# Cross-attention with a routed expert layer: four early expert tiles taken from six routed token tiles instead of three from four, with a new instruction order

## The reference

```
x1 = x + attention(layernorm(x), ctx, mask) @ Wo + bo
h = layernorm(x1)                                  # 1024 x 128
probs = softmax(h @ w_gate + b_gate)               # 8 experts
p, e = max(probs), argmax(probs)
out = x1 + p * (relu(h @ W1[e] + b1[e]) @ W2[e] + b2[e])   # 128 -> 512 -> 128
```

| tokens routed | tokens of expert 0 to 7 | full tiles of 128 with one expert |
|---|---|---|
| first 4 tiles (512) | 140, 9, 31, 132, 9, 8, 9, 174 | 3 |
| first 6 tiles (768) | 140, 9, 39, 323, 13, 44, 24, 176 | 4 |
| all 8 tiles (1024) | 147, 9, 64, 465, 19, 54, 88, 178 | 5 |

## Time and profile before

### The profile page before, as it was taken

One profiled execution on the slowest core, in us unless ns is written; L12 is line 12 of the kernel. 1 busy time (PEld: TensorE's weight loads), 2 busy tenths in 40 slices (PEclk: granted clock), 3 DMA queues, 4 the chain that ended last, 5 costly groups with the idle time before them and its releaser, 6 DMA issues.

```text
span 122.6 us, 2830 instructions
## 1 busy us (share of the span) xinstructions
PE 99.6 (81%) x770; PEld 79.4 (65%) x770; DVE 74.3 (61%) x255; ACT 75.4 (62%) x377; POOL 53.7 (44%) x85
## 2 busy tenths in 40 slices
PE   4599899979799999999888889986319999799700
PEld 4376665426558888856785579975209999689600
DVE  0551687664869979569766766567725266656600
ACT  0603855998579998789895998545003675474300
POOL 7730003067009683063886324152780056467560
PEclk9999999999999999999999999999955899999995
DMA  2999999999999930000010200000142222200010
GB/s 80 350 350 263 288 275 275 275 276 212 373 353 293 298 133 3 0 0 5 14 55 22 66 8 0 22 22 8 47 108 69 66 69 58 71 29 14 23 34 5
DMA packets 17624, 15.06 MB, mean 123 GB/s; under 512 B 1288, under 2 KB 14772, under 8 KB 17600
## 3 DMA queue, kind: packets, MB, share of 16 engines
q1 hardware_dynamic: 16096, 11.99, 37.9%
q10 hardware_dynamic: 704, 1.70, 3.8%
q0 software_dynamic: 800, 1.10, 2.8%
HBM read 8.92 MB, written 6.19 MB: 123 GB/s over the span
## 4 chain that ended last, share of the span: by engine, by line
PE 46%; DVE 14%; issue 10%; ACT 9%; POOL 7%; DMA 7%; DVEq 1%; ACTq 1%; POOLq 0%; SPq 0%
PE bank L996 11%; ACT probs L694 8%; PE bank L876 6%; PE bank L973 6%; PE bank L1191 5%; POOL out_x L570 4%; DMA w_qkv<-in_L_xattn_Wk 4%; PE bank L982 4%; PE bank L923 3%; PE bank L948 3%; PE bank L886 2%; DMA regions<-token_rows,row_of 2%; PE bank L970 2%; DVE neg_max L1468 1%; DMA vo<-regions 1%
## 5 line engine op out<-in xcount | busy, mean ns | idle before, releaser
L694 ACT ACTIVATE probs<-bank,neg_max 128x64 f32<-128x64 f32 x128 | 38.0, 346 | 2.6 <-DVE neg_max L1468 1.9
L694 ACT ACTIVATION_READ_ACCUMULATOR probs<-bank,neg_max 128x1 f32 x128 | 30.5, 240 | 0.0
L533 POOL TENSOR_TENSOR probs<-probs,inv_sum 128x512 f32<-128x512 f32 x16 | 16.6, 1042 | 23.3 <-DVE inv_sum L1474 23.3
L629 ACT ACTIVATE w_qkv<-bank,b_stage 128x128 f32<-128x128 f32 x52 | 14.8, 367 | 9.7 <-PE bank L876 9.7
L996 PE MATMUL bank<-vo,probs_T 128*128 128x128 f32 x128 | 16.6, 278 | 0.8 <-DVE vo L1462 0.5
L996 PEld LDWEIGHTS bank<-vo,probs_T 128*128 128x128 f32 x128 | 15.3, 192 | 2.7 <-issue 1.6
L570 POOL DMA_INDIRECT out_x<-vo,token_of x10 | 10.4, 1037 | 13.9 <-DVE vo L1633 9.2
L973 PE MATMUL bank<-zero_padded,normed_T 128*128 128x512 f32 x32 | 16.3, 592 | 0.0
L886 PE MATMUL bank<-w_sb,w_qkv 128*128 x104 | 14.3, 281 | 0.8 <-ACT w_qkv L629 0.4
L886 PEld LDWEIGHTS bank<-w_sb,w_qkv 128*128 128x128 f32 x104 | 12.8, 193 | 1.4 <-issue 1.3
L876 PE MATMUL bank<-vo,w_qkv 128*128 128x128 f32 x80 | 12.6, 308 | 1.4 <-DVE w_qkv L1624 0.9
(11 more groups left out here) (159 smaller groups left out, 172.1 us busy)
## 6 DMA issues: line engine op xcount, KB each, us to landing
regions<-empty_row SPq DMA_DIRECT2D x1, 4224.0 KB, 23.0
w_sb<-in_L_ffn_W SPq DMA_DIRECT2D x1, 2048.0 KB, 26.5
vo<-regions SPq DMA_DIRECT2D x15, 66.0 KB, 1.8
x_tok<-in_x SPq DMA_DIRECT2D x2, 256.0 KB, 4.8
w_qkv<-in_L_xattn_Wk ACTq DMA_DIRECT2D x1, 512.0 KB, 4.6
w_qkv<-in_L_xattn_Wq ACTq DMA_DIRECT2D x1, 512.0 KB, 5.9
w_qkv<-in_L_xattn_Wv ACTq DMA_DIRECT2D x1, 512.0 KB, 6.8
wo_sb<-in_L_xattn_Wo SPq DMA_DIRECT2D x1, 512.0 KB, 7.6
```

The lines of the kernel that those rows point to most:

```text
L533: pool.tensor_tensor(p, p, inv, ALU.mult).then_inc(short["multiply"], 1)
L629: act.activation(hidden[:, i % 2, c * P:(c + 1) * P], banks[i % 2][:, c * P:(c + 1) * P], ACT.Relu, bias=b1_stage[:, i % 3, c:c + 1]).then ...
L694: last = act.activation(probs[:, n % 2, g, c], score_bank_of(h)[:, c], ACT.Exp, bias=neg_max[:, n % 2, g, i:i + 1], accum_out=row_sum[:, n ...
```

## The change

- `ROUTED` becomes four groups: tiles 6 and 7 are routed one by one.
- `EARLY_GROUPS = 2`, `EARLY = 4`: the early table is made after six token tiles, for four early tiles. All early work stands later in the list, and the late tiles begin at number 4.
- `SHORT_STEPS` is written in a new order, for all of attention as well.
- The token index is stored as integer bits, and the scatter of a result reads its offsets straight from the loaded row: the casts on POOL and their semaphore go.
- `WARM` is 2 and not 4. `early_stage` of tile 3 reuses staging buffer 0 and waits for tile 0's relu. `late_constants` is followed by a wait for itself.
- The program for a full mask, which does not run here, does its early work after attention.

```
-    EARLY_GROUPS = 1
-    EARLY = 3
+    EARLY_GROUPS = 2
+    EARLY = 4
-    ROUTED = [[0, 1, 2, 3], [4, 5], [6, 7]]
+    ROUTED = [[0, 1, 2, 3], [4, 5], [6], [7]]
-    WARM = 4
+    WARM = 2
         SHORT_STEPS = """
...
-        gates 0 | turn_drain.s 9 | turn 10 | vo_drain.s 2 0 | place 0 | vo_drain.v 2 1 | out 8 | turn_drain.s 10
-        exp 12 | multiply 11 | out 9 | exp 13 | early_table | scatter 0 0 | x1 4 | scatter 0 1 | turn 11 | inverse 12
-        scatter 0 2 | out 10 | scatter 0 3 | turn_drain.v 11 | out 11 | early_stage 0 | row_statistics 4 | multiply 12
-        score 14 | x1 5 | h_T 1 | turn 12 | inverse 13 | row_statistics 5 | ln2 1 | h_drain.v 1 | logits 1 | h_power 1
-        max 14 | turn_drain.s 12 | score 15 | choose 1 | max 15 | exp 14 | rank 1 | multiply 13 | rank_drain 1 | turn 13
-        vo 3 | inverse 14 | gates 1 | turn_drain.s 13 | multiply 14 | vo_drain.v 3 1 | vo_drain.s 3 0 | exp 15 | turn 14
-        out 12 | early_slots 0 | turn_drain.v 14 | early_turn 0 | out 13 | early_slots 1 | inverse 15 | early_turn 1
-        early_turn_drain 0 | x1 6 | early_slots 2 | place 1 | late_constants | multiply 15 | early_turn_drain 1
-        early_hidden 0 | early_stage 1 | early_relu 0 | out 14 | turn 15 | turn_drain.v 15 | early_turn 2
-        row_statistics 6 | early_hidden 1 | out 15 | x1 7 | early_result 0 | scatter 1 0 | early_relu 1 | h_T 2
-        row_statistics 7 | h_drain.s 2 | ln2 2 | early_result 1 | logits 2 | h_power 2 | early_stage 2 | early_finish 0
-        early_finish 1 | choose 2 | early_turn_drain 2 | gates 2 | scatter 1 1 | early_hidden 2 | rank 2 | rank_drain 2
-        place 2 | counts | early_relu 2 | early_result 2 | late_table | early_finish 2 | scatter 2 0 | scatter 2 1
...
+        score 3 | x_power 1 | inverse 0 | exp 1 | score 4 | multiply 0 | exp 2 | inverse 1 | x_normalise 1 | multiply 1
...
+        inverse 11 | gates 0 | score 14 | turn_drain.s 9 | vo_drain.v 2 0 | place 0 | turn_drain.v 10 | max 13
+        vo_drain.s 2 1 | multiply 11 | scatter 0 0 | exp 12 | out 8 | out 9 | turn 11 | x1 4 | turn_drain.v 11 | exp 13
+        max 14 | row_statistics 4 | out 10 | out 11 | scatter 0 1 | exp 14 | scatter 0 2 | inverse 12 | x1 5 | h_T 1
+        row_statistics 5 | ln2 1 | scatter 0 3 | multiply 12 | h_drain.v 1 | turn 12 | inverse 13 | logits 1 | score 15
+        h_power 1 | inverse 14 | choose 1 | max 15 | gates 1 | turn_drain.s 12 | rank 1 | exp 15 | rank_drain 1
+        place 1 | multiply 13 | early_counts | early_counts_read | turn 13 | vo 3 | vo_drain.v 3 1 | vo_drain.s 3 0
+        turn_drain.s 13 | inverse 15 | multiply 14 | turn 14 | scatter 1 0 | out 12 | out 13 | scatter 1 1 | early_table
+        x1 6 | multiply 15 | row_statistics 6 | turn_drain.s 14 | ln2 2 | turn 15 | turn_drain.s 15 | h_T 2
+        h_drain.s 2 | h_power 2 | out 14 | logits 2 | out 15 | choose 2 | early_stage 0 | x1 7 | h_T 3 | early_slots 0
+        row_statistics 7 | rank 2 | ln2 3 | early_turn 0 | h_drain.v 3 | gates 2 | logits 3 | rank_drain 2
+        early_turn_drain 0 | h_power 3 | early_stage 1 | choose 3 | place 2 | early_stage 2 | early_slots 1 | gates 3
+        early_hidden 0 | counts | rank 3 | rank_drain 3 | early_turn 1 | early_relu 0 | place 3 | late_constants
+        early_turn_drain 1 | early_slots 2 | early_result 0 | scatter 2 0 | late_table | scatter 3 0 | early_turn 2
+        early_hidden 1 | early_stage 3 | early_turn_drain 2 | early_slots 3 | early_hidden 2 | early_relu 1
+        early_finish 0 | early_turn 3 | early_turn_drain 3 | early_result 1 | early_finish 1 | early_relu 2
+        early_hidden 3 | early_relu 3 | early_result 2 | early_result 3 | early_finish 2 | early_finish 3
         """
...
-            pool.memset(empty_row[:, :, INDEX], float(N)).then_inc(more_consts, 1)
+            pool.memset(empty_row[:, :, INDEX].bitcast(I32), N).then_inc(more_consts, 1)
...
-            def token(i):
+            def scatter_result(i):
                 pool.wait_ge(tile_loaded[i], 16)
-                pool.tensor_copy(token_of[:, i:i + 1], rows_at(i, slice(INDEX, INDEX + 1))).then_inc(tokens_ready, 1)
-
-            def scatter_result(i):
-                pool.wait_ge(tokens_ready, i + 1)
                 pool.wait_ge(result_ready, i + 1)
-                pool.indirect_dma_start(out=out_rows, out_offset=bass.IndirectOffsetOnAxis(ap=token_of[:, i:i + 1], axis=0),
+                pool.indirect_dma_start(out=out_rows, out_offset=bass.IndirectOffsetOnAxis(ap=rows_at(i, slice(INDEX, INDEX + 1)).bitcast(I32), axis=0),
...
+                if i >= 3:
+                    act.wait_ge(relu_done, HC * (i - 2))
-                act.activation(b1_stage[:, i, :].unsqueeze(1),
+                act.activation(b1_stage[:, i % 3, :].unsqueeze(1),
...
-                        late_constants()
+                        after(late_constants())
```

More of the change, by code:

```diff
@@ L286, in xattn_moe @@
-        score 11 | row_statistics 2 | inverse 9 | exp 10 | h_drain.s 0 | turn_drain.s 8 | row_statistics 3 | ln2 0
-        max 11 | logits 0 | h_power 0 | score 12 | exp 11 | choose 0 | score 13 | max 12 | rank 0 | multiply 9
-        inverse 10 | early_counts | multiply 10 | rank_drain 0 | inverse 11 | turn 9 | early_counts_read | vo 2 | max 13
-        gates 0 | turn_drain.s 9 | turn 10 | vo_drain.s 2 0 | place 0 | vo_drain.v 2 1 | out 8 | turn_drain.s 10
-        exp 12 | multiply 11 | out 9 | exp 13 | early_table | scatter 0 0 | x1 4 | scatter 0 1 | turn 11 | inverse 12
@@ new lines, in xattn_moe @@
+        inverse 8 | row_statistics 1 | score 10 | turn 7 | max 10 | exp 9 | multiply 8 | turn_drain.s 7 | out 6
+        row_statistics 2 | inverse 9 | out 7 | x1 3 | exp 10 | turn 8 | h_T 0 | score 11 | h_drain.s 0
+        row_statistics 3 | ln2 0 | multiply 9 | h_power 0 | logits 0 | inverse 10 | score 12 | max 11 | turn 9
+        choose 0 | multiply 10 | score 13 | rank 0 | turn_drain.v 8 | rank_drain 0 | max 12 | turn 10 | exp 11 | vo 2
+        inverse 11 | gates 0 | score 14 | turn_drain.s 9 | vo_drain.v 2 0 | place 0 | turn_drain.v 10 | max 13
@@ L581, in scatter_from @@
                 with pool.Else():
-                    if i + 1 < ALL:
-                        token(i + 1)
                     scatter_result(i)
@@ L592, in _ @@
             for i in range(EARLY):
-                token(i)
-            for i in range(EARLY):
                 scatter_result(i)
```

103 lines of the change are left out of this document (39 added, 64 removed).

## The result

| | us |
|---|---|
| before, in the same set of runs | 125.45 median (123.97 to 126.76) |
| changed | 129.67 median (129.24 to 131.41, 4 runs) |
| ratio | 1.0435 (95% interval 1.0367 to 1.0503) |
| changed, profiled execution | 129.47, span 127.4, 2.07 outside it (before 1.75) |
| mean granted clock | 0.917 (before 0.962) |

Ratios compare fast runs alone; single executions of the same kernel can be 1.5% and more slower, the medians here take such executions in, and the profiles of warm_all, port_free and table_ahead are of such executions.

What follows compares the result with a forecast made beforehand. PE was taken as busiest engine, with one hole ahead of the late tiles; afterwards the early tiles become the bound. Tile 6 starting at 96.4 instead of 98.97 gains 2.6, so 124.35 becomes 121.7 us, 8-in-10 range 119.8 to 124.8.

Steps and rivals of the forecast that it cites:

- Attention up to x1 7: Attention to its last output: ready at 78.5 instead of 79.13, a gain of 0.6; 77.9 at best.
- What exp 15 waits for: ACT's last exp in attention: waits for turn 12's drain and max 15, both near 69.2; ends at 71.6, some 2.4 earlier.
- The port: DVE normalising beside POOL's multiply 1: shared-port blocking makes max 3 and exp 3 about 1.0 later, covered by ACT's idle time.
- The table in front of x1 6: Rival in late attention: exp 15 as late as before, the 2.8 us table puts x1 7 at 80.4; 123.6, chance 0.15.
- if PE's idle time before x1 7 grows with the early work gone: Sign in attention that would show the prediction wrong; no size given.
- From x1 7, once ready, to the last scatter: Routing of the last tile behind attention: 4.9 instead of 7.1, last scatter at 83.4.
- The late table and loads: Behind the last scatter: first late load at 86.2, landed at 88.0 instead of 90.54, but nobody there to take it.
- The early tiles: Four early tiles on PE, ACT and DVE become the bound; first late hidden product at 93.3, against 92.29 before.
- The relay rival: Between 84 and the first late tile: early tiles don't overlap, 9.9 instead of 6.5; 125.1, chance 0.1.
- What is gained in the end: Late tiles: one fewer, first to third hidden product 3.05 at full clock, tile 6 at 96.4 instead of 98.97; gain 2.6.
- The clock as a rival: PE's hole ahead of the late tiles: clock falls, 4.74 for 3.05, costing 1.7; 123.4, chance 0.2.
- Edits at nothing: Casts, integer bits, the new wait and WARM: casts hidden, bits nothing, wait under 0.1, WARM's 0.3 in PE's idle time.

Runs made afterwards that it cites:

- warm_all: The changed kernel with idle PE products put in front of PE's waits and WARM 16 instead of 2; ratio 1.0433.
- port_free: The changed kernel with place 0 ahead of the drains of vo 2 and inverse 13 and 14 behind choose 1; 131.87 against 125.55.
- table_ahead: The changed kernel with early_table moved right behind early_counts_read, ahead of the drains of vo 3; ratio 1.0261.
- the second profile: Profile of the same changed kernel, nothing altered, run again later; 127.56 median against 126.11 for the kernel before.

## Why the prediction was wrong

**1. Attention up to x1 7** is the step that failed. It was to be ready at 78.5 and was ready at 82.77 (start 82.43), which is 4.3 of the 7.8 us by which tile 6's hidden product missed its 96.4. The sum had inverse 15 end at 71.8; it ended at 75.80, behind the late drain of vo 3. The table then took 0.4 more than its 2.8, and x1 6 waited 0.45 for out 13. That is 4.9 on top of the best case of 77.9. From x1 6 to x1 7 the sum held.
- *"behind the first group's four scatters on POOL as before"*: not as before. Place 0 now stands behind a drain of vo 2, the scatters came 1.57 later (59.48 to 61.05), and multiply 12 with them, beside `var_eps`.
- *What exp 15 waits for* (71.70, forecast 69.2). The sum had max 15 and the drain of turn 12, both near 69.2. Max 15 stands behind choose 1 and ended at 71.20. Turn 12 was done at 67.86, but gates 1, which the sum left out, stands ahead of turn 12's drain on ACT and needs choose 1 too. So exp 15 follows the one-hot, and that came 1.56 later than before.
- *The port.* I weighed the rule of the Trainium skill (SBUF — State Buffer, "Who interferes with whom") at multiply 1 only, where it was covered. There four instructions took 1.80 for 1.10, and x1 0 came no later than before (40.70 for 41.25). It struck at `var_eps`, 0.70 for 0.17, and at choose 1, which I had at its old length: 0.36 became 1.27. port_free gave both back. The second was to be read off the new list: multiply 13 and 14 had their inputs, so they would run beside it.
- *The hand-over of vo 3* (a drain from 71.16 to 75.00). vo 3 started 2.0 later, 1.56 of it with the one-hot. Another 1.8 came on top, and the scatters beside it suffice for that: the drain followed the end of the second one by 0.60, and by 0.57 in the second profile, where vo 3 ran at full clock. Nothing in my sum stood for either.
- *The table in front of x1 6* was a rival at 123.6, and its condition came true: exp 15 was as late as before. It had x1 7 ready at 80.4, 2.4 earlier than measured, since it knew nothing of the drain of vo 3. The table costs 0.9 to 1.1 when the clock is up; where it isn't, the half-speed products cover it.

I had named "if PE's idle time before x1 7 grows with the early work gone" as what would make me wrong, and gave it no price. The clock of this stretch fell behind these waits in both profiles.

**2. From x1 7, once ready, to the last scatter**: 4.9 forecast, 4.73 measured. The working was right, single routing and all.

**3. The late table and loads**: first load 91.33, 3.83 behind the last scatter for my 2.8, and it lay idle until DVE normalised it at 98.43, as forecast.

**4. The early tiles**: from the last scatter to hidden 3, 4.3 forecast, 6.11 at half clock and 4.69 in the profile at full clock. The relay rival (in turn, 3.4 more) didn't come.

**5. What is gained in the end**: first to third late hidden product 3.05 forecast, 4.54 in the first profile, 3.00 in the second. There were nine late results as forecast, and a late tile took 1.93 to 1.97 on PE (1.94 forecast).

**The clock as a rival** had 0.2 and one fall of 1.7. The fall it named, in the hole ahead of the late tiles, came in one profile of two and cost what it said (4.54 for 3.00, 1.5). What it missed are the other falls: one on the early tiles, 1.4 more, and one in attention, where I had looked for none. Behind x1 7 alone the clock is worth 2.9.

**Edits at nothing.** The casts: the scatter still starts with the result, so they were hidden as I said, yet the part by itself costs about 2%. If parts add up, that is about half of the 4.35%. That they do is not shown: of the part's 2%, only 0.3 us outside the span and up to 1 us in the first late tiles repeat.

**The slower side.** The only rival that I priced for it, the relay, lay behind x1 7. The largest loss lay ahead of it, in a stretch that I let come out late in one case only, that of the table.

## What to carry to other kernels

Where work that filled PE's waits is moved away, price the clock at each wait it leaves, not only at the longest: here it fell behind several of 0.9 to 1.5 us, close together. When an order is rewritten, list for each step on the critical path everything that stands ahead of it on its own engine, as gates 1 stood ahead of exp 15. Go through the new list for every DVE step that now has a GpSimd operation with ready inputs beside it, and give each chain ahead of the moved part a time of its own. An edit that only touches constants and a hidden cast still deserves a run by itself; here it alone made the kernel some 2% slower, for a reason that stays open.
